# Windowed attention block on one Trainium2 core: new orders for all engines, another dealing of three PSUM banks, and K and Q transfers issued one pass nearer to their producers

## The reference

```python
xn = layernorm(xw) * ln_g + ln_b                        # xw: windows, 49 tokens, 96 channels
q, k, v = split(xn @ qkv_w.T + qkv_b)                   # 12 heads of 8
attn = softmax(q * 8**-0.5 @ k.T + bias_table[REL_IDX]) # 49 x 49 for a window and a head
seq = x + (attn @ v) @ proj_w.T + proj_b
s2 = batchnorm(depthwise_conv3x3(seq))                  # over the image, padding 1
out = s2 + gelu(s2 @ w1.T + b1) @ w2.T + b2             # hidden 384
```

## Time and profile before

| | |
|---|---|
| time, median of 3 runs | 3547.06 us (3522.06 to 3551.41) |
| the profiled execution: its time, its span | 3537.58 us, 3535.8 us |
| mean granted TensorE clock | 0.986 |
| PE busy, PEld busy | 3183.9 us (90%), 2137.9 us (60%) |
| DVE, ACT, POOL busy | 3005.9 us (85%), 2833.1 us (80%), 1154.8 us (33%) |
| DMA: data queues of SP and POOL | 22.8% and 7.1% of 16 engines |
| instructions | 209261, of which 93452 matmuls and 93452 weight loads |

### The profile page before, as it was taken

How to read it: one execution, slowest core, us unless ns; L and a number is a source line. 1 busy time by engine, 2 the same in 40 slices (tenths; PEclk the granted TensorE clock), 3 DMA queues, 4 the chain that set the end, 5 groups by cost and what they waited for, 6 DMA issues and landing times.

```text
span 3535.8 us, 209261 instructions
## 1 busy us (share of the span) xinstructions
PE 3183.9 (90%) x93452; PEld 2137.9 (60%) x93452; DVE 3005.9 (85%) x5161; ACT 2833.1 (80%) x4887; POOL 1154.8 (33%) x1550
## 2 busy tenths in 40 slices
PE   3899998999999999899999999998999999899997
PEld 2566665666666666566666666665666666666663
DVE  4788888888888888888888888888888888888885
ACT  3788877887888888778888888887888888888785
POOL 2333333333333333333333333333333333333331
PEclk9999999999999999999999999999999999999997
DMA  1333333333333333333333333333333333333331
GB/s 41 93 95 94 95 94 91 97 88 95 96 94 99 91 95 98 87 94 94 96 97 91 96 98 90 97 91 94 96 90 99 96 93 95 96 90 99 89 92 36
DMA packets 269954, 322.64 MB, mean 91 GB/s; under 512 B 55651, under 2 KB 252580, under 8 KB 269062
## 3 DMA queue, kind: packets, MB, share of 16 engines
q1 hardware_dynamic: 236294, 232.12, 22.8%
q0 software_dynamic: 32768, 77.14, 7.1%
HBM read 39.35 MB, written 38.54 MB: 22 GB/s over the span
## 4 chain that ended last, share of the span: by engine, by line
PE 52%; DMA 18%; SPq 17%; DVE 6%; issue 5%; ACT 1%; POOL 1%; ACTq 0%; DVEq 0%; POOLq 0%
PE a_ps L250 18%; DMA k_all<-kh 18%; SPq L208 15%; PE d_ps L250 8%; PE sm_ps L309 8%; PE o_ps L334 7%; PE st_ps L288 6%; PE b_ps L250 6%; DVE mx L682 3%; DVE kl L716 2%; SPq L202 2%; ACT sq L528 0%; SPq L189 0%; POOL ox L604 0%; DVE s L708 0%
## 5 line engine op out<-in xcount | busy, mean ns | idle before, releaser
L708 DVE SCALAR_TENSOR_TENSOR s<-ximg,cols,s 96x392 f32<-96x392 f32 x2048 | 1268.6, 619 | 27.7
L682 DVE TENSOR_REDUCE mx<-sm_ps 128x12 f16<-128x588 f32 x1024 | 788.0, 770 | 345.8 <-PE sm_ps L309 337.1
L462 ACT ACTIVATE p<-st_ps 128x588 f32<-128x588 f32 x1024 | 664.2, 649 | 127.4 <-PE st_ps L288 120.8
L604 POOL DMA_DIRECT2D ox<-o_sb x1024 | 581.0, 570 | 557.2 <-ACT o_sb L487 508.7
L309 PEld LDWEIGHTS sm_ps<-k_all,q_all 127*49 127x49 f16 x24576 | 472.4, 104 | 440.9 <-DMA k_all<-kh 243.4
L592 POOL TENSOR_TENSOR s<-ximg,cols 96x392 f32<-96x392 f32 x256 | 277.5, 1084 | 1144.8 <-DVE y L745 1144.8
L309 PE MATMUL sm_ps<-k_all,q_all 127*49 127x49 f16 x24576 | 524.1, 187 | 137.3 <-DMA k_all<-kh 116.7
L250 PE MATMUL a_ps<-g,w_s 128*64 128x392 f32 x3072 | 626.3, 515 | 3.6 <-ACT g L513 3.1
L288 PE MATMUL st_ps<-q_all,k_all 128*49 128x49 f16 x24576 | 524.4, 186 | 76.7 <-issue 69.6
L288 PEld LDWEIGHTS st_ps<-q_all,k_all 128*49 128x49 f16 x24576 | 450.2, 104 | 127.8 <-issue 105.4
L584 POOL TENSOR_TENSOR xl<-xn,xh 96x392 f16<-96x392 f32 x256 | 276.7, 1081 | 651.0 <-ACT xh L543 650.8
(11 more groups left out here) (103 smaller groups left out, 5144.8 us busy)
## 6 DMA issues: line engine op xcount, KB each, us to landing
ox<-o_sb POOLq DMA_DIRECT2D x1024, 73.5 KB
k_all<-kh SPq DMA_DIRECT2D x512, 96.0 KB
q_all<-qh SPq DMA_DIRECT2D x512, 96.0 KB
x_sb<-in_x SPq DMA_DIRECT2D x256, 147.0 KB, 3.6
out<-y SPq DMA_DIRECT2D x256, 147.0 KB, 3.9
k_all<-kl SPq DMA_DIRECT2D x256, 96.0 KB
q_all<-ql SPq DMA_DIRECT2D x256, 96.0 KB
q_all<-mxt SPq DMA_DIRECT2D x256, 12.0 KB, 2.1
```

The costliest lines, as they stand in the source:

```text
L462: af(p32[:, p, :, :].rearrange("p (b h) n -> p b h n", b=2), st_ps[:, :, 0:HALF].rearrange("p b (h n) -> p b h n", n=TOK), ACT.Exp).then_i ...
L604: nc.gpsimd.dma_start(ox[:, c % 2, x4, :], o_sb[x4::4, c % 2, :, :]).then_inc(o_in[c % 2], 16)
L682: v.tensor_reduce(mx[:, c % 2, :, p].rearrange("p (b h) -> p b h", b=2), sm_ps[:, :, 0:HALF].rearrange("p b (h n) -> p b h n", n=TOK), AX. ...
L708: v.scalar_tensor_tensor(acc, image_rows(c, k // 3, k % 3), cw_c[:, k:k + 1], acc, ALU.mult, ALU.add)\
```

## The change

Only calls are reordered, given another lag, or given another PSUM bank. Every function does the same work.

- SP: in a step the last K transfer, the store, the load and the maximum row come first, then five K/Q transfers of chunk s - 2 (before: of s - 3, with the load after the first of them), in the order K low, Q high, K high, Q low, Q high.
- PE: a new order and new lags (variance s - 1, values s - 3, exp_scores 2 of s - 4, max_scores 3 of s - 3, projection s - 6).
- Banks: queries from b_ps to a_ps, second from a_ps to b_ps, hidden 0 on d_ps and hidden 1 on b_ps.
- ACT: exp 3 and inverses move behind gelu, query_high to the end of the step of its own chunk.
- POOL: to_channels first, then first_tap, then input_low.
- DVE: four taps in a row, key_low and query_low in the step of their own chunk.

```diff
@@ sync
             for s in range(STEPS):
-                first_term(k_all, 1, kl, kl_done, s - 3)
-                load(s)
-                term(k_all, 0, kh, kh_done, s - 3)
-                term(q_all, 0, qh, qh_done, s - 3)
-                term(q_all, 1, qh, qh_done, s - 3)
-                term(q_all, 2, ql, ql_done, s - 3)
                 term(k_all, 2, kh, kh_done, s - 3)
                 store(s - 10)
+                load(s)
                 maximum_row(s - 4)
+                first_term(k_all, 1, kl, kl_done, s - 2)
+                term(q_all, 1, qh, qh_done, s - 2)
+                term(k_all, 0, kh, kh_done, s - 2)
+                term(q_all, 2, ql, ql_done, s - 2)
+                term(q_all, 0, qh, qh_done, s - 2)
@@ tensor: values_times_p, free and first wait
-                if p == 1:
+                if p == 0:
                     wait(pe, v32_done, c)
...
-                elif p == 2:
+                elif p == 3:
                     free(pe, (o_done[0], c+0), (o_done[1], c-1))
@@ queries
-                wide_three(b_ps[0:128, 0:CT], wq_h[:, 0:128], ...
+                wide_three(a_ps[0:128, 0:CT], wq_h[:, 0:128], ...
@@ hidden, second
-            hidden_ps = {0: b_ps, 1: d_ps, 2: a_ps}
+            hidden_ps = {0: d_ps, 1: b_ps, 2: a_ps}
...
-                wide(a_ps[0:128, 0:CT], w2_s[:, k, :], g[:, k, :], start=k == 1, stop=k == 2).then_inc(s_done[k], 1)
+                wide(b_ps[0:128, 0:CT], w2_s[:, k, :], g[:, k, :], start=k == 1, stop=k == 2).then_inc(s_done[k], 1)
@@ the order of PE, new (the old one stands in words above)
+                variance(s - 1)
+                values(s - 3)
+                exp_scores(s - 4, 2)
+                values_times_p(s - 4, 0)
+                max_scores(s - 3, 3)
+                projection(s - 6)
+                hidden(s - 8, 1)
                 hidden(s - 8, 0)
+                hidden(s - 8, 2)
                 maxima_rows(s - 3)
+                second(s - 8, 1)
+                exp_scores(s - 4, 3)
+                second(s - 8, 0)
+                keys(s - 1)
                 max_scores(s - 2, 0)
+                queries(s - 1)
+                second(s - 8, 2)
+                max_scores(s - 2, 1)
                 values_times_p(s - 4, 1)
+                centred(s)
                 exp_scores(s - 3, 0)
+                max_scores(s - 2, 2)
+                values_times_p(s - 4, 3)
                 values_times_p(s - 4, 2)
                 exp_scores(s - 3, 1)
@@ scalar
-                inverses(s - 5)
-                exp(s - 4, 3)
                 outputs(s - 4, 0)
-                query_high(s - 1)
                 exp(s - 3, 0)
...
                 gelu(s - 7, 1)
                 input_high(s)
+                gelu(s - 7, 0)
                 gelu(s - 7, 2)
-                gelu(s - 7, 0)
                 act.preload_act_table_set("natural_log_exp_and_others")
+                exp(s - 3, 3)
                 log_sums(s - 4)
                 key_high(s)
+                inverses(s - 4)
+                query_high(s)
@@ gpsimd
+                to_channels(s - 4)
+                first_tap(s - 6)
                 input_low(s)
-                first_tap(s - 5)
-                to_channels(s - 3)
@@ vector: the new order
+                tap(s - 7, 8)
+                maxima(s - 2, 2)
+                values_out(s - 2)
+                input_normal(s)
+                image_sum(s - 5)
+                maxima(s - 2, 3)
+                tap(s - 6, 1)
+                maxima_out(s - 2)
+                tap(s - 6, 2)
+                tap(s - 6, 3)
+                tap(s - 6, 4)
+                tap(s - 6, 5)
+                maxima(s - 1, 0)
+                key_low(s)
+                tap(s - 6, 6)
+                maxima(s - 1, 1)
+                query_low(s)
+                normalise(s - 4)
+                tap(s - 6, 7)
+                block_out(s - 7)
```

More of the change, by code:

```diff
@@ L341, in centred @@
                 wait_ring(pe, x_in, c)
-                free(pe, (kl_done, c-1), (g_done[1], c-8), (xn_done, c-1))
+                free(pe, (kl_done, c-1), (g_done[0], c-8), (xn_done, c-1))
                 at = c % CPI * CT
@@ L372, in values @@
                 wait(pe, xl_done, c)
-                free(pe, (ql_done, c+1), (g_done[0], c-6), (v32_done, c-1))
+                free(pe, (y_done, c-6), (g_done[1], c-6), (v32_done, c-1))
                 for n in range(NP):
@@ L384, in projection @@
                 wait(pe, norm_done, c)
-                free(pe, (lnv_done, c+5), (y_done, c-3), (g_done[2], c-3), (sum_done, c-1))
+                free(pe, (lnv_done, c+5), (ql_done, c+4), (g_done[2], c-3), (sum_done, c-1))
                 for w in range(2):
@@ L412, in second @@
                 if k == 1:
-                    free(pe, (g_done[2], c+0), (sum_done, c+2), (lnv_done, c+7), (y_done, c-1))
-                wide(a_ps[0:128, 0:CT], w2_s[:, k, :], g[:, k, :], start=k == 1, stop=k == 2).then_inc(s_done[k], 1)
+                    free(pe, (g_done[1], c+0), (v32_done, c+5), (y_done, c-1))
+                wide(b_ps[0:128, 0:CT], w2_s[:, k, :], g[:, k, :], start=k == 1, stop=k == 2).then_inc(s_done[k], 1)
             for s in range(STEPS):
+                variance(s - 1)
[5 more added lines that the diff above has]
+                hidden(s - 8, 1)
                 hidden(s - 8, 0)
-                hidden(s - 8, 1)
+                hidden(s - 8, 2)
                 maxima_rows(s - 3)
-                hidden(s - 8, 2)
+                second(s - 8, 1)
+                exp_scores(s - 4, 3)
+                second(s - 8, 0)
+                keys(s - 1)
                 max_scores(s - 2, 0)
-                exp_scores(s - 4, 3)
+                queries(s - 1)
+                second(s - 8, 2)
+                max_scores(s - 2, 1)
                 values_times_p(s - 4, 1)
-                values_times_p(s - 4, 0)
-                second(s - 8, 1)
-                keys(s - 1)
-                max_scores(s - 2, 1)
-                second(s - 8, 0)
-                second(s - 8, 2)
-                queries(s - 1)
+                centred(s)
                 exp_scores(s - 3, 0)
+                max_scores(s - 2, 2)
+                values_times_p(s - 4, 3)
                 values_times_p(s - 4, 2)
-                values_times_p(s - 4, 3)
-                max_scores(s - 2, 2)
-                centred(s)
-                values(s - 2)
                 exp_scores(s - 3, 1)
-                variance(s)
-                max_scores(s - 2, 3)
-                exp_scores(s - 3, 2)
-                projection(s - 5)
         @block.scalar
@@ L483, in outputs @@
                     return
-                wait(act, pv_done[0 if half == 0 else 3], c)
+                wait(act, pv_done[1 if half == 0 else 2], c)
                 if half == 0:
@@ L733, in values_out @@
                 wait(dve, v_done, c)
-                wait(dve, pv_done[3], c - 2)
+                wait(dve, pv_done[2], c - 2)
                 v.tensor_tensor(v32[:, c % 2, :, :, :].rearrange("p h n (d x) -> p (h n d) x", x=4)[:, :, 0:2],
```

41 lines of the change are left out of this document (13 added, 28 removed).

## The result

The changed kernel takes 3505.85 us (median of 8 runs, 3503.95 to 3516.67), the kernel before 3539.36 us beside it: ratio 0.9903, 95% interval 0.9875 to 0.9931. So it became faster by 1.0%, where I had forecast 3695 us and given 0.72 to slower and 0.08 to a change within 1%. The profiled execution took 3510.61 us.

What follows compares the result with a forecast made beforehand. PE was taken as the bound, with transfer waits and instruction-packet stalls. Terms -0.65 + 1.2 + 0.05 = +0.6 us a step, +154 us over 256 steps on 3537.6: 3692, stated 3695 us; range 3590 to 3840, 8-in-10 range 3440 to 3840.

Steps and rivals of the forecast that it cites:

- rival 1: Instruction fetches stay covered, stalls hold at 0.7 us a step, only (a) and (c) count: 3385 to 3395 us; chance 0.2.
- What bounds the kernel now: PE, busy 90% of a 13.33 us step, with waits for K/Q transfers and "issue" stalls at instruction packet ends.
- (a): K/Q transfers, issued nearer their producers and needed later: the transfer wait goes, gain 0.65 us a step (0.46 to 0.95).
- margin of 1.4 us: K/Q landing 11 us after keys start, against 12.4 us or more until max_scores needs it.
- (b): Instruction pieces on PE: small-matmul blocks laid together use pieces up faster, stalls 0.8 to 2.0, cost 1.2 us a step.
- (c): New orders on ACT and DVE: four narrow places for PE's waits, cost 0.05 us a step, 0 to 0.3.
- four narrow places: PE's exp_scores 1, next variance, max_scores 2 and max_scores 3, each barely supplied in time by ACT or DVE.
- (d): PSUM bank changes: new frees come from readers ending early enough; no cost, up to 0.3 us if cover is gone.
- (e): first_tap, to_channels and their DMAs on POOL, stores on SP: nothing, up to 0.2 us.
- The first and last ten steps change by a few us: Start and end of the run: a few us either way, outside the sum per step.
- rival 2: Stalls grow, but only to 1.4 us a step, cancelling the transfer gain: 3530 to 3570 us; chance 0.08.

Runs made afterwards that it cites:

- a_spold: The changed kernel with SP's old list (load behind the first K transfer, old order of the six transfers): 3521.21 us, ratio 0.9912.
- a_drift: The changed kernel with 25 semaphore increments a step on PE (767 instructions), so piece ends move by one instruction a step: 3618.13 us, 1.02.
- a_dve: The changed kernel with two convolution taps later on DVE, one behind key_low, one behind maxima 1: 3469.84 us, 0.977.
- a_pair: The changed kernel with value product 0 moved ahead of value product 1, so both stand together: 3561.16 us, 1.0031.
- a_lock48: The changed kernel with 26 semaphore increments a step on PE, fixing piece ends at exp_scores 3, exp_scores 0 and in values: 3517.43 us, 0.9907.
- a_lock200: As a_lock48, with piece ends 152 instructions further (max_scores 1, exp_scores 1, end of max_scores 3): 3788.14 us, 1.0675.
- a_thin: The changed kernel with each K/Q transfer cut from 96 to 12 KB: 3500.58 us, 0.9849.
- b_drift: The kernel before with 25 semaphore increments a step on PE (767 instructions), so piece ends move by one instruction a step: 3657.29 us, 1.0306.
- b_sp: The kernel before with SP's load moved behind the six K/Q transfers: 3475.53 us, 0.9791.
- b_swap: b_sp with max_scores 0 behind exp_scores 3 and the value products, and DVE's tap 4 ahead of maxima 0: 3469.84 us, 0.9766.
- b_lock248: The kernel before with 26 increments a step on PE, fixing piece ends at hidden 1, max_scores 1 and late max_scores 2: 3850.34 us, 1.0848.

## Why the prediction was wrong

The forecast had a loss of 0.6 us a step; it became a gain of 0.05, and the range of 3590 to 3840 us was missed by 84 us. The wider one, 3440 to 3840, holds the time only since it reached down towards rival 1.

**What bounds the kernel now** was read rightly: piece ends cost 0.75 us a step, the transfers 0.46 to 0.95.

**(a), gain 0.65: right,** 0.63 in front of max_scores 0, and 0.2 more spread over the step. The margin of 1.4 us was there as well: the old SP list costs nothing in the new order (a_spold). The sign of the forecast did not depend on it.

**(b), cost 1.2: the step that failed**, measured 0.20. It read: "So from entering a piece to being able to enter the next one, L = 4.3 us here; other stalls give 3.8 to 4.3. I take 4.1", and used that for every place of the new order. The density was right (39% of the starting places are used up in about 2.5 us), and the stalled ends went up from 212 to 307 of 710, at the places forecast (a_drift). But they did not get longer: 0.90 us in the mean before, 0.79 after, where a latency of 4.1 would give 1.6 inside the dense run. Taken apart, L is the time until the next piece's transfer begins, the transfer, about 1.1 us, and about 1.4 us from its end until PE goes on. The last two are much the same in all kernels. The first varies: between the 10th and the 90th percentile, stalled pieces of the kernel before have 1.0 to 2.5 us, L 3.7 to 5.3 (median 4.0, so that the 4.1 was right for it), of the changed kernel 0.6 to 1.6 us, L 3.0 to 4.2 (median 3.5). I had read L from stalls of one order and carried it to another as if it were a property of the chip. With L = 3.5 the same sum gives 2.9 x (0.39 x 1.0 + 0.13 x 0.4) = 1.3 us for the new order in place of 2.0; measured is 0.95, a cost of 0.20 in place of 1.2. That is 256 us of the forecast. So the shorter L explains two thirds of the error; the rest of it stays open.

**(c), cost 0.05: mis-sized,** measured 0.58. Half of it (0.30) is the wait for the maximum of block 0 behind four taps. My walk through the step found four narrow places and not this one; a_dve shows it by taking it away. A tap also became longer, from 619 ns in the mean in the kernel before to 655 ns in the row above; over eight taps that is 0.29 us of DVE a step. The other half (0.28) is a cost that I had at nothing: the change splits the value products, and that has a price. A value product that follows a block of scores starts 0.41 to 0.43 us after it, where another block of scores or a wide product starts after 0.32 to 0.34; two value products in a row take 0.65 us, one alone 0.40. a_pair shows 0.26 for one that is split off. Before a wide product, which is float32 too, nothing is added, so the type alone isn't shown to be the reason.

**(d) and (e): nothing, as forecast.** "The first and last ten steps change by a few us" was too small: 15 us at the end, half of the whole gain.

**The sum closes, and luck is in it.** Against the forecast's steps, (b) is 1.0 us a step less, (a) gives 0.18 more and (c) costs 0.53 more: 0.65 us, 166 us in 256 steps. With the 15 us at the end that is, to 1 us, the distance from the 3692 us forecast for the profiled execution to its 3510.6. Without the opposite error of (c) the miss would have been over 300 us.

**The rivals.** The outcome lies nearest to rival 2 (stalls grow less, and the rest cancels), to which I gave 0.08, 24 us under its 3530 to 3570. But its sum isn't what happened: it had stalls grow by 0.6, they grew by 0.20, and what cancelled the gain was mostly (c). Rival 1 was nearer in the stalls and wrong in the price: its gain was there, and was eaten by (c) and the rest of (b). I had weighed the Trainium skill ("Runtime: NRT & Kernel Launch", section Instruction fetch mechanics), which has a boundary mostly hidden. The runs speak against "mostly hidden" for this kernel (0.95 us a step of stalls here, and a_lock48 against a_lock200, 271 us), though its cost here moved by 0.2 us a step, not 1.2. My error was to take knowing that the rule is wrong here for knowing by how much.

**What stays open** is what sets the delay before the next piece is asked for. Not the K and Q traffic (a_thin). Not the place alone and not the increments alone (the drifts, and a_lock48). It is no fixed time and no fixed number of instructions behind the entry: the 10th and 90th percentile are 0.66 and 2.28 us in the kernel before, 0.97 and 2.86 in b_drift. What a piece begins with has a part: in the kernel before, b_sp and b_swap the third of the stalled pieces whose first 64 instructions take longest (1.5 to 2.1 us) has a median delay of 2.1 to 2.6 us, the other two thirds 1.2 to 1.5; in the changed kernel the thirds have 0.9, 1.1 and 1.1. The increments among these first instructions seem to have one too (b_drift). Whether the history counts beside them was not tried.

## What to carry to other kernels

Before an order of all engines is drawn anew, try the one cheap move on the chain that the profile names: the load behind the transfers gave 75 us here, the whole new order 34, and after two small repairs of its DVE list 107 (each beside the kernel before in its own group of runs). Count a program's instructions per loop against 256, since a stream of small matmuls pays at piece ends, by an amount that must be measured for each order; a latency read from the stalls of one order is no constant for another. And do the walk through the step for every wait of the bound engine, also those far from the ones that the change was meant for.

## What the runs showed of the hardware

- Where an instruction piece ends is worth up to 271 us of 3517 with the same instructions in each step (a_lock48, a_lock200), 16 of them once at the start.
- A piece at a stalled end takes about 1.1 us to transfer and 1.4 us more until PE goes on, in every kernel; the time until its transfer begins goes from 0.6 to over 3 us (in b_drift 3.35 us in the mean of the ends near place 208), and isn't shortened by cutting the DMA load from 92 to 55 GB/s.
- The kernel before stalls 0.75 us a step with ends that slide by 26 instructions; with 26 increments and fixed ends (b_lock248) two ends cost 0.69 + 1.47 = 2.16 us. That the ends stand still isn't shown to be the reason, since increments among a piece's first instructions go with a later transfer.
- 26 semaphore increments a step behind wide products on PE lengthen the step by under 0.05 us where the stalls stay the same (a_lock48: 13.29 us against 13.28). In a row ahead of the loop they start 0.15 us apart.
- Splitting a value product (24 small float32 matmuls) off its pair and setting it between blocks of float16 scores costs PE 0.26 us: the block of scores ahead takes 0.41 us in place of 0.32, and two value products take 0.40 us each apart, 0.65 together. Whether the type or the shape does it was not tried.
